# Second edge layer of a graph network: destination rows spread by a backward scan instead of gathered

## The chip, the cores and the metric

One core of one Trainium2 chip. The metric is the device time of one launch in microseconds (us). The kernel before was timed three times: median 6531.28 us, from 6530.24 to 6546.5 us.

## The reference, cut to what matters

100,000 nodes with 96 features in f32, 50,000 edges. The edges come **sorted by destination**, so all edges into one node stand next to each other (a run). Four graph layers follow one another, each in the form `x = x + layer(relu(norm(x)))`; the fourth is a stack of three convolutions with one norm and one skip around it. The first two layers have an MLP on every edge; the second is the one that changes here:

```python
# second edge layer, h = relu(layernorm(x))
e = jnp.concatenate([h[src], h[dst]], axis=-1)
e = jax.nn.relu(e @ Wm1 + bm1) @ Wm2 + bm2
e = e * drop_mask                                  # edge_attr_96
m = jax.ops.segment_sum(e, dst, num_segments=n)
z = jnp.concatenate([h, m], axis=-1)
h_new = jax.nn.relu(z @ Wu1 + bu1) @ Wu2 + bu2
```

`h[dst]` is one row per run: every edge of a run has the same destination row, normed in the same way.

## The kernel before, in words

All work goes in **groups** of 512 rows: four tiles of 128 partitions by 96 features. Nodes that no edge points to need no messages; they are handled for all nodes alike in a **node pass** (phase `dn`, 196 groups), which writes its rows to the tables `t1` and `t2` behind row `E_PAD` = 50,176. Nodes with edges are handled in edge order: 98 groups of 512 edges, in each layer. The table rows below `E_PAD` belong to edges: the row at the **last** edge of a run holds the right state of its destination node after each layer (the sum over a run is complete there), the rows at other edges hold values that nobody looks up. So to find a node's current row one needs a translation from node number to table row, `info_d` (row, and degree factor).

The stages in order:

- Counting (0 to 515 us): degrees and the translation table are built.
- Node pass `dn` (515 to 2105 us): per group a dense load, norm, MLP, norm, MLP, three stores. Beside it, on GpSimd, `info_gather` looks up two groups of 128 edges per step: four gathers of 8 bytes per row from `info_d` into `got` (two for the sources, `which` 0, two for the destinations, `which` 1) and two gathers of source rows of `x`. The found numbers are kept in `found`.
- First edge layer `e0` (2105 to 2927 us), not changed in its work.
- Second edge layer `e1` (2927 to 3935 us), lines 657 to 677 (GpSimd), 793 to 850 (ScalarE), 963 to 1045 (TensorE), 1324 to 1401 (VectorE). Per group eight gathers on GpSimd: four of source rows into `xs`, four of destination rows into `xd`, both from `t1`.
- Four convolution passes `conv` (3935 to 6548 us), each bound to gathers of its own.

Within `e1` a group j runs through: moments of `xs` and `xd` (`edge_moments`), `rstd` and `nmr` by eleven tiny instructions (`roots`), ScalarE norms into `hs` and `hd`, TensorE transposes both (`tr`, L973 and L978), ScalarE copies them out of PSUM into `hsT` and `hdT` (`evac_s`, `evac_d`), TensorE computes the hidden layer (`hid`, L990 from `hsT`, L992 from `hdT`), ScalarE applies relu (L828), TensorE makes messages (L1007), VectorE multiplies with the mask (`times_drop`, L1349), TensorE turns the messages (L1015), VectorE sums runs by a forward scan (`sums`, L1317; the factor `goes` is 1 where an edge has the destination of the edge before it, and 0 where a run begins), TensorE computes the update (`upd_z`, L1023 from `hdT`, L1024 from `aggT`; `upd_u`, L1031), and VectorE adds it to the edge's own row `xn` (`new_x`, L1381), which SyncE loads from `t1` in edge order (`res`).

The order on each engine is fixed by `pipelined(engine, n, stages)`: in step i an engine does its stages in the order of the list, each for group i minus its lag. No scheduler moves anything; an instruction waits for its semaphores and everything behind it on its engine waits with it. Before, `e1` has these lists: TensorE `hid` 1, `upd_z` 3, `turn_messages` 2, `messages` 1, `upd_u` 3, `tr` 0; ScalarE `evac_d` 1, `hidden` 1, `update_act` 3, `norms` 0, `evac_s` 0; VectorE `times_drop` 2, `new_x` 4, `edge_moments` 0, `of_round` (roots) 0, `sums` 2; GpSimd and SyncE run ahead as far as buffers allow (`xs`, `xd`, `xn`: six, `goes`, `drop`: three).

Of the kernel before, what the change touches and what calls it, by code (L numbers as in the profile page):

```python
# [6 lines left out]
F16 = mybir.dt.float16  # L7
# [4 lines left out]
P = 128  # L12
D = 96
# [78 lines left out]
def half(g):  # L92

    return g.c // GT % 2
# [24 lines left out]
def build(nc, a, out):  # L119
    with ExitStack() as ctx:  # L120
# [12 lines left out]
        goes_d = dram("goes_d", (E_PAD,), F16)  # L133
# [44 lines left out]
        at = sb("at", [P, 7, ET], I32)  # L178
        found = sb("found", [P, 2, ET, 2])
# [4 lines left out]
        off = sb("off", [HI, 1])  # L184


        idx = sb("idx", [P, 2, 2, GT * G], I32)
        idx_out = sb("idx_out", [P, 2, GT * G], I32)
        got = sb("got", [P, 2, 2, GT * GI, 2])
# [28 lines left out]
        goes = sb("goes", [P, 3, GE], F16)  # L218
# [48 lines left out]
        idx_step = sem("idx_step")  # L267
        rows_found = sem("rows_found")
# [26 lines left out]
        def more(name, k, by):  # L295
# [6 lines left out]
                        got=(2, 2 * GI * GT, GT), kept=(2, 1, GT), xs=(6, GI, 1), c_out=(6, 1, 1)))  # L302
        dn["root"] = Count(sem("root_dn"))
        gathered = dict(idx_in=(2, 1, GT), xs=(6, G, 1), goes=(3, 1, 1), x_out=(3, 1, 1))
        edge_slots = dict(gathered, xd=(6, G, 1), attr=(3, 1, 1))
        e0 = Phase(EG, dict(mx=1, norm_s=1, norm=1, tr_s=1, tr=1, evac_s=1, evac=1, hid_g=1, hid=1, act_g=1, act=1,
                            tok_g=1, tok=1, gate=1, msg=1, agg=1, z=1, g=1, u=1, y=1, my=1, norm_y=1, yx=1, xb=1, xr=1),
                   {name: edge_slots[name] for name in edge_slots if name != "xs"} | dict(x_in=(6, 1, 1)))
# [55 lines left out]
        def _(sp):  # L364
# [5 lines left out]
            sp.wait_ge(pad_set, 3)  # L370
# [10 lines left out]
            sp.wait_ge(scratch_out, 64)  # L381
            sp.dma_start(st_p[:], dstp[0:E_PAD].rearrange("(p t) -> p t", t=ET)).then_inc(prev_in, 16)
# [26 lines left out]
            sp.dma_start(goes_d.rearrange("(p t) -> p t", t=ET), st_goes[:]).then_inc(goes_out, 16)  # L409
# [6 lines left out]
            def idx_columns(ph, g, n, per, planes):  # L416
                k = per * (GT if g.turn is not None else min(GT, n - g.j))
                sp.dma_start(idx[:, half(g), 0:planes.stop - planes.start, 0:k], at[:, planes, bass.ds(g.j * per, k)])\
                    .then_inc(ph["idx_in"][half(g)].sem, 16)

            def info_idx(g):
                if g.c % GT == 0:
                    need(sp, dn["got"][half(g)], freed(g, 6, 2 * GI * GT))
# [5 lines left out]
                    idx_columns(dn, g, NG, GI, slice(0, 2))  # L429

            def info_keep(g):
                last = is_last_group(g, NG)
                if g.c % GT == GT - 1 or last:
                    n = g.c % GT + 1
                    need(sp, dn["got"][half(g)], freed(g, 6, 2 * GI * GT) + 16 * 2 * GI * n)
                    sp.sem_inc(sp_turn, 1)
                    sp.dma_start(found[:, :, bass.ds((g.j - n + 1) * GI, n * GI), :].rearrange("p w e c -> p w (e c)"),
                                 got[:, half(g), :, 0:n * GI, :].rearrange("p w e c -> p w (e c)"))\
# [35 lines left out]
            def gather_idx(ph, planes):  # L474
# [1036 lines left out]
```

## Time and profile before

| | |
|---|---|
| runs | 6531.28 us median, 6530.24 to 6546.5 |
| span of the profiled execution | 6548.3 us (the page gives no other time of it) |
| PE, weight load | 4333.9 us busy (66%), 2863.0 us (44%) |
| VectorE | 3928.1 us (60%) |
| ScalarE | 3505.9 us (54%) |
| GpSimd | 4163.7 us (64%), 4323 instructions |
| DMA | 620.32 MB, mean 95 GB/s |

No engine is busy throughout, because the stages have different limits. Read one stage at a time: a table of windows, one per stage, then who waits for whom in that stage, then the timeline of one or two groups. A stage is bound by the engine that waits for nothing there; "issue" as the releaser of a wait means that the engine was only between two of its own instructions. PEclk is the granted TensorE clock as a share of 2.4 GHz; it has two levels, 1.00 and 0.50, and a mean between them tells how the time was shared. TensorE's f32 products are issued as two instructions each, so "x8" in its rows are four products.

### The profile page before, as it was taken

Reading aid. Unit: us, or ns where it says so; the run is one execution under the profiler, and the core shown is the slowest. Engines: PE = TensorE matmul, PEld = TensorE weight load, DVE = VectorE, ACT = ScalarE, POOL = GpSimd, SP = SyncE. Lnnn points to the kernel's source line nnn. Section 1 sums busy time; section 2 is a strip of 40 time slices with the busy share of each in tenths; the row PEclk is TensorE's granted clock in tenths of the full one; section 3 lists DMA queues with packets and bytes.
Section 4 is the critical chain, followed back from the end, with each engine's and each line's share of the span. In section 5 each row is a group of like instructions: output and inputs, shape, how many; then the busy total and the mean of one; then the engine's idle time right before and its main releaser. Section 6 shows DMA issues by size and latency. Waiting matters only on the chain. (4 is left out here: it accounts for less than half of the span.)

```text
span 6548.3 us, 106418 instructions
## 1 busy us (share of the span) xinstructions
PE 4333.9 (66%) x19614; PEld 2863.0 (44%) x19614; DVE 3928.1 (60%) x12722; ACT 3505.9 (54%) x8822; POOL 4163.7 (64%) x4323
## 2 busy tenths in 40 slices
PE   5777888888887999978788884554555555222222
PEld 2224655655664444434444443443444444222222
DVE  5666777777776888875555555665665443222222
ACT  6996888888886999975555552222222222111110
POOL 0006777777775544437777767775775776777777
PEclk9997888898888999987888885555555555555555
DMA  0003444444444333434444444554444999333332
GB/s 16 0 0 90 124 126 127 125 128 125 124 124 119 93 96 93 96 72 100 111 107 111 107 100 120 136 134 96 104 104 90 103 104 100 62 62 66 70 66 58
DMA packets 1058872, 620.32 MB, mean 95 GB/s; under 512 B 831285, under 2 KB 1004609, under 8 KB 1058778
## 3 DMA queue, kind: packets, MB, share of 16 engines
q1 hardware_dynamic: 920794, 450.66, 25.2%
q0 software_dynamic: 137984, 168.67, 17.2%
q14 instruction: 67, 0.55, 0.0%
q8 instruction: 27, 0.44, 0.0%
HBM read 368.86 MB, written 251.78 MB: 95 GB/s over the span
## 5 line engine op out<-in xcount | busy, mean ns | idle before, releaser
L629 POOL DMA_INDIRECT xs<-t,idx x1176 | 1110.2, 944 | 528.4 <-issue 349.1
L629 POOL DMA_INDIRECT got<-info_d,idx x784 | 788.9, 1006 | 776.7 <-issue 750.1
L1048 PE MATMUL bank<-ident,msg 128*96 128x128 f32 (+1 forms) x1568 | 424.8, 426 | 1047.0 <-ACT msg L872 872.6
L1055 PE MATMUL bank<-w,aggT 96*128 96x96 f32 (+1 forms) x3136 | 770.2, 426 | 400.8 <-DVE aggT L1317 400.5
L629 POOL DMA_INDIRECT xs<-c,idx x784 | 749.8, 956 | 296.5 <-issue 233.0
L1055 PEld LDWEIGHTS bank<-w,aggT 96*128 96x128 f32 (+1 forms) x3136 | 704.4, 329 | 503.0 <-issue 422.9
L872 ACT ACTIVATE msg<-xs,now 128x96 f32<-128x96 f32 x784 | 229.4, 363 | 1279.8 <-DMA xs<-c,idx 840.0
L1048 PEld LDWEIGHTS bank<-ident,msg 128*96 128x96 f32 (+1 forms) x1568 | 285.7, 216 | 1113.3 <-ACT msg L872 738.5
L1317 DVE TENSOR_TENSOR_SCAN aggT<-goes,aggT,bank 96x512 f32<-96x512 f16 (+1 forms) x490 | 621.2, 1268 | 102.3 <-PE bank L1015 34.6
L629 POOL DMA_INDIRECT xd<-in_x_dram,idx x392 | 374.9, 956 | 415.8 <-DVE xn L1366 228.3
L725 ACT ACTIVATE hd<-xd,nmr,rstd 128x96 f32<-128x96 f32 x1568 | 599.3, 455 | 27.5 <-DVE nmr L1206 27.5
L1462 DVE SCALAR_TENSOR_TENSOR y<-bank,now,rows 128x96 f32<-128x96 f32 x392 | 97.2, 311 | 699.0 <-PE bank L1055 699.0
L711 POOL DMA_INDIRECT out_dram<-xn,idx_out x392 | 390.0, 995 | 119.3 <-issue 119.0
L629 POOL DMA_INDIRECT xs<-in_x_dram,idx x392 | 377.3, 962 | 119.5 <-issue 118.6
L629 POOL DMA_INDIRECT xd<-t,idx x392 | 369.9, 944 | 119.5 <-issue 119.5
L1462 DVE SCALAR_TENSOR_TENSOR xn<-bank,now,rows 128x96 f32<-128x96 f32 x784 | 194.5, 311 | 406.7 <-PE bank L1055 394.5
L899 PE MATMUL bank<-xd,hot_hi 128*128 128x392 f16 x1568 | 324.0, 328 | 124.3 <-ACT hot_hi L737 116.0
L1117 DVE TENSOR_SCALAR xd<-iota_lo,lo_of 128x784 f16<-128x784 f16 x784 | 297.0, 421 | 143.1 <-PE bank L899 143.0
L725 ACT ACTIVATE hs<-xs,nmr,rstd 128x96 f32<-128x96 f32 x784 | 300.6, 456 | 135.2 <-DVE nmr L1206 135.0
L1231 DVE BATCH_NORM_STATS2 mv<-xs 128x6 f32<-128x192 f32 x392 | 122.2, 353 | 415.8 <-issue 217.0
L912 PE MATMUL bank<-hdT,uw 96*96 96x512 f32 x392 | 253.9, 734 | 175.8 <-ACT hdT L770 175.8
L932 PEld LDWEIGHTS bank<-uw,u 97*128 97x128 f32 x1568 | 279.0, 218 | 178.3 <-ACT u L775 109.2
(189 smaller groups left out, 10436.4 us busy)
## 6 DMA issues: line engine op xcount, KB each, us to landing
t<-xo SPq DMA_DIRECT2D x392, 192.0 KB
t<-xn SPq DMA_DIRECT2D x294, 192.0 KB, 2.2
goes<-goes_d SPq DMA_DIRECT2D x392, 128.0 KB
xd<-in_x_dram SPq DMA_DIRECT2D x196, 192.0 KB, 2.5
out_dram<-oo SPq DMA_DIRECT2D x196, 192.0 KB, 2.4
xd<-t SPq DMA_DIRECT2D x196, 192.0 KB, 3.5
c<-xn SPq DMA_DIRECT2D x196, 192.0 KB
x_src<-xs SPq DMA_DIRECT2D x196, 96.0 KB
```

The lines of the kernel that those rows point to most:

```text
L629: nc.gpsimd.indirect_dma_start(out=into, out_offset=None, in_=table, in_offset=bass.IndirectOffsetOnAxis(ap=indices, axis=0)).then_inc(don ...
L711: nc.gpsimd.indirect_dma_start(out=out[:, :], out_offset=bass.IndirectOffsetOnAxis(ap=idx_out[:, half(g), col + c:col + c + 1], axis=0), i ...
L725: ins = nc.scalar.activation(into[:, c, :], x[:, c, :], ACT.Relu, bias=nmr[:, b, q, c:c + 1], scale=rstd[:, b, q, c:c + 1])
L872: ins = nc.scalar.activation(msg[:, g.at(2), c, 0:D], xs[:, g.at(6), c, :], ACT.Relu, scale=scale[:, col + c:col + c + 1])
L899: ins = nc.tensor.matmul(bank[1 + 2 * which + side][0:HI, 0:SIDE], hot_hi[:, g.at(2), which, 0:HI], hot_lo[:, g.at(2), which, side * SIDE: ...
L912: nc.tensor.matmul(into, w, x, start=True, stop=True).then_inc(done.sem, 1)
L932: nc.tensor.matmul(to, u1[:, g.at(2), e], uw2[:], start=True, stop=False)
L1048: ins = nc.tensor.transpose(bank[g.at(2)][0:m, c * P:(c + 1) * P], msg[:, g.at(2), c, 0:m], ident[:])
L1055: ins = nc.tensor.matmul(tok(bank[2 + g.at(2)], m)[:, c, :], aggT[0:m, g.at(3), c * P:(c + 1) * P], w2[:] if k == 0 else w3[:, k - 1, :], ...
L1117: nc.vector.tensor_scalar(hot_lo[:, g.at(2), which, :], iota_lo[:], lo_of[:, which, bass.ds(g.j, 1)], None, ALU.is_equal).then_inc(hot, 1)
L1317: nc.vector.tensor_tensor_scan(aggT[0:m, s, :], goes[0:m, s, :], source(g), aggT[0:m, before, GE - 1:GE], ALU.mult, ALU.add)\
L1462: ins = nc.vector.scalar_tensor_tensor(out=to, in0=u[:, c, 0:D], scalar=now[:, half(g), 1, col + c:col + c + 1], in1=rows[:, 1 + k, :], op ...
```

## The change

The destination look-ups and gathers go. Since the edges are sorted, the state of the destination of every edge of a run is the table row at the run's last edge, and that row is among the rows that `e1` loads in edge order anyway (`xn`, the row to which the update is added). So:

- `edge_moments` and the second half of `norms` read `xn` instead of `xd`. After `rstd` is made, a twelfth instruction multiplies it with `is_last`, and `nmr` is made from the product: relu(0·x + 0) = 0, so `hd` has the normed row at the last edge of each run and zeros elsewhere.
- After the transpose, `evac_d` on ScalarE is gone; VectorE's new stage `spread` writes `hdT` by a scan that goes **backward** over the 512 edges of the group: `hdT[i] = goes[i+1] * hdT[i+1] + bank[i]`. A run's row is thus carried back to all its edges. The scan starts from `carry[:, j]`, the normed row with which a run that goes on past the end of group j has to start.
- `carry` (96 by 98) is made once before `e1`: one gather of 98 rows of `info_d` at the start of the node pass, one gather of 98 rows of `t1` before the first gather of `e1`, moments and roots over 98 rows (`end_pass`: 13 small VectorE instructions), one norm, one transpose, one copy.
- `goes` in `e1` is loaded one column wider (513). In SyncE's list `res_load` moves to lag 1 (it was part of `edge_load`, lag 3) and `goes_load` from lag 5 to lag 2.
- GpSimd has four gathers per group in `e1` (before eight), and four per step in the node pass (before six); its wait for a free buffer is now on `norm_s` alone. Index tiles shrink to one plane; `found` and `got` too.

VectorE in the middle of `e1`, one step from its last roots instruction on, before (`mv` are the moments, `bank` a PSUM bank, `aggT` the running sums):

```order
L1206 SCALAR_TENSOR_TENSOR nmr<-mv,rstd 128x12
L1317 SCALAR_TENSOR_TENSOR aggT<-goes,aggT,bank 96x512
L1349 TENSOR_TENSOR msg<-bank,drop 128x4x96
L1381 TENSOR_TENSOR xo<-xn,bank 128x384
L1231 BN_STATS mv<-xs 128x6 x2
L1231 BN_STATS mv<-xd 128x6 x2
L1184 TENSOR_SCALAR var<-mv 128x12
```

and with the change:

```order
L1247 SCALAR_TENSOR_TENSOR rstd<-sq,root 128x12
L1252 TENSOR_TENSOR rstd<-rstd,is_last 128x4
L1254 SCALAR_TENSOR_TENSOR nmr<-mv,rstd 128x12
L1367 SCALAR_TENSOR_TENSOR aggT<-goes,aggT,bank 96x512
L1420 TENSOR_TENSOR msg<-bank,drop 128x4x96
L1451 TENSOR_TENSOR xo<-xn,bank 128x384
L1280 BN_STATS mv<-xs 128x6 x2
L1280 BN_STATS mv<-xn 128x6 x2
L1402 SCALAR_TENSOR_TENSOR hdT<-goes,carry,bank 96x512
L1228 TENSOR_SCALAR var<-mv 128x12
```

Moved: one small instruction (L1252) stands ahead of `nmr`, the moments read `xn`, and the scan `hdT` of the group before (L1402) stands between the moments and the roots of the new group. This listing names both scans SCALAR_TENSOR_TENSOR; in the trace they are TENSOR_TENSOR_SCAN.

ScalarE in the middle of `e1`, one step, before (`m` is the hidden layer's relu, `u` the update's):

```order
L809 ACTIVATE hsT<-bank 96x512
L814 ACTIVATE hdT<-bank 96x512
L828 ACTIVATE m<-bank,bias 96x512
L840 ACTIVATE u<-bank,bias 96x512
L725 ACTIVATE hs<-xs,nmr,rstd 128x96 x4
L725 ACTIVATE hd<-xd,nmr,rstd 128x96 x4
L809 ACTIVATE hsT<-bank 96x512
```

and with the change:

```order
L755 ACTIVATE hs<-xs,nmr,rstd 128x96 x4
L755 ACTIVATE hd<-xn,nmr,rstd 128x96 x4
L846 ACTIVATE hsT<-bank 96x512
L865 ACTIVATE m<-bank,bias 96x512
L877 ACTIVATE u<-bank,bias 96x512
L755 ACTIVATE hs<-xs,nmr,rstd 128x96 x4
L755 ACTIVATE hd<-xn,nmr,rstd 128x96 x4
```

Moved: the copy `hdT` is gone, so nothing of ScalarE stands between `hsT` and `m`; `u` stays ahead of the two norms `hs` and `hd`.

The diff, cut to its core:

```diff
-        goes_d = dram("goes_d", (E_PAD,), F16)
+        goes_d = dram("goes_d", (E_PAD + 1,), F16)
...
# SyncE
+            sp.dma_start(end_dst[:], dstp[1:1 + E_PAD].rearrange("(g e) -> g e", e=GE)[:, GE - 2:GE]).then_inc(ends_in, 16)
...
-                    if ph is e1:
-                        sp.dma_start(xn[:, g.at(6), :, :], edge_view(t1, first)).then_inc(ph["res"][g.at(6)].sem, 16)
+                def res_load(g):
+                    need(sp, ph["xr"], g.j - 5)
+                    sp.sem_inc(sp_turn, 1)
+                    sp.dma_start(xn[:, g.at(6), :, :], edge_view(t1, g.j * GE)).then_inc(ph["res"][g.at(6)].sem, 16)
...
+                if ph is e0:
+                    stages = [(gather_idx(ph, plane), 0), (xs_load, 1), (edge_load, 3), (goes_load, 5), (edge_store, done)]
+                else:
+                    stages = [(gather_idx(ph, plane), 0), (res_load, 1), (goes_load, 2), (edge_load, 3), (edge_store, done)]
# GpSimd
+            nc.gpsimd.indirect_dma_start(
+                out=end_info[:], out_offset=None, in_=info_d[:, :],
+                in_offset=bass.IndirectOffsetOnAxis(ap=end_dst[:, 1:2], axis=0)).then_inc(ends_found, 16)
...
-                for which in range(2):
-                    for c in range(col, col + GI):
-                        gather(got[:, half(g), which, c, :], info_d[:, :], idx[:, half(g), which, c:c + 1],
-                               dn["got"][half(g)])
+                for c in range(col, col + GI):
+                    gather(got[:, half(g), c, :], info_d[:, :], idx[:, half(g), c:c + 1], dn["got"][half(g)])
...
+                    nc.gpsimd.indirect_dma_start(
+                        out=end_x[:], out_offset=None, in_=t1[0:E_PAD, :],
+                        in_offset=bass.IndirectOffsetOnAxis(ap=end_at[:, 0:1], axis=0)).then_inc(end_rows, 16)
...
-                    need(pool, ph["norm"], g.j - 5)
+                    need(pool, ph["norm"] if ph is e0 else ph["norm_s"], g.j - 5)
...
-                    for c in range(G if ph is e1 else 0):
-                        gather(xs[:, g.at(6), c, :], t[:, :], idx[:, half(g), 0, col + c:col + c + 1], ph["xs"][g.at(6)])
-                    which = 1 if ph is e1 else 0
+                    into, done = (xd, ph["xd"]) if ph is e0 else (xs, ph["xs"])
                     for c in range(G):
-                        gather(xd[:, g.at(6), c, :], t[:, :], idx[:, half(g), which, col + c:col + c + 1], ph["xd"][g.at(6)])
+                        gather(into[:, g.at(6), c, :], t[:, :], idx[:, half(g), col + c:col + c + 1], done[g.at(6)])
# ScalarE
-                    normed(hd[:, g.at(6), :, :], xd[:, g.at(6), :, :], g.at(3), 1).then_inc(ph["norm"].sem, 1)
+                    normed(hd[:, g.at(6), :, :], (xd if first else xn)[:, g.at(6), :, :], g.at(3), 1)\
+                        .then_inc(ph["norm"].sem, 1)
...
-                    pipelined(act, EG, [(evac_d, 1), (hidden, 1), (update_act, 3), (norms, 0), (evac_s, 0)])
+                    pipelined(act, EG, [(hidden, 1), (update_act, 3), (norms, 0), (evac_s, 0)])
# VectorE
+                if masked is not None:
+                    part, mask = masked
+                    v.tensor_tensor(part, part, mask, ALU.mult).then_inc(count.sem, 1)
+                    need(dve, count, before + 11)
...
+                def spread(g):
+                    need(dve, ph["tr"], g.j + 1)
+                    need(dve, ph["goes"][g.at(3)], landed(g, 3))
+                    need(dve, ph["z"], g.j - 5)
+                    dve.sem_inc(dve_turn, 1)
+                    nc.vector.tensor_tensor_scan(hdT[0:D, g.at(6), ::-1], goes[0:D, g.at(3), 1:GE + 1][:, ::-1],
+                                                 bank[1][0:D, ::-1], carry[:, bass.ds(g.j, 1)], ALU.mult, ALU.add)\
+                        .then_inc(ph["evac"].sem, 1)
...
-                    stages = [(times_drop, 2), (new_x, 4), (edge_moments, 0), (of_round, 0), (sums, 2)]
+                    stages = [(times_drop, 2), (new_x, 4), (edge_moments, 0), (spread, 1), (of_round, 0), (sums, 2)]
```

## Rows read from the trace of the kernel before

**Rows 1.** Windows, one per stage: start:end, length, busy us (instructions), PEclk, DMA, GB/s
```profile
515.00:2105.00 1590.00, 1338.46 (x7056) 942.01 (x7056) 1194.30 (x4356) 1278.69 (x3137) 1166.19 (x1176) 0.86 0.43 123
2105.00:2927.00 822.00, 716.50 (x2744) 351.28 (x2744) 709.16 (x2305) 755.56 (x1764) 374.85 (x392) 0.98 0.38 91
2927.00:3935.00 1008.00, 813.93 (x3528) 472.45 (x3528) 515.10 (x1765) 527.50 (x1176) 739.85 (x784) 0.84 0.43 106
3935.00:4480.00 545.00, 290.97 (x1174) 250.01 (x1174) 353.10 (x1239) 144.04 (x392) 369.83 (x392) 0.50 0.54 130
```

**Rows 2.** Groups of GpSimd, second edge layer, 2990 to 3830 us: busy, mean ns, idle
```profile
L629 POOL DMA_INDIRECT xd<-t,idx x336 | 317.1, 944 | 102.4 <-issue 102.4
```

**Rows 3.** Timeline: both ends of the second edge layer
```profile
2927.21 0.94 POOL L629 DMA_INDIRECT xs<-t,idx  x1 [70.67 <-DMA idx<-at]
...
2938.70 0.63 DVE L1231 BATCH_NORM_STATS2 mv<-xs 128x6 f32<-128x192 f32 x2 [14.51 <-DMA xd<-t,idx]
...
3909.46 0.63 DVE L1231 BATCH_NORM_STATS2 mv<-xs 128x6 f32<-128x192 f32 x2 [5.48 <-issue]
...
3935.54 0.94 POOL L629 DMA_INDIRECT xs<-t,idx  x1 [29.84 <-DMA idx<-at]
```

**Rows 4.** Waits in the second edge layer, 2990 to 3830 us: total us, times, longest
```profile
DVE mv L1231 <- DMA xd<-t,idx: 146.4, 35, 5.7
```

**Rows 5.** Waits in the node pass, 700 to 1900 us
```profile
DVE mv L1231 <- PE bank L933: 198.6, 149, 4.1
...
POOL got L629 <- DMA found<-got: 18.0, 8, 4.9
```

**Rows 6.** Waits of the DMA queue SP in the same stretch
```profile
SPq L443 <- DVE xn L1258: 496.2, 126, 7.5
SPq L428 <- DMA xs<-in_x_dram,idx: 89.1, 47, 2.6
```

**Rows 7.** Timeline, node pass: the first product of two groups in succession
```profile
1202.69 1.10 PE L912 MATMUL bank<-hdT,uw 96*96 96x512 f32 x2 [1.12 <-ACT hdT L770]
...
1210.04 1.10 PE L912 MATMUL bank<-hdT,uw 96*96 96x512 f32 x2 [1.12 <-ACT hdT L770]
```

**Rows 8.** Timeline, second edge layer at full clock: start, length, engine, instruction, count
```profile
3410.99 0.69 ACT L840 ACTIVATE u<-bank,bias 96x512 f32<-96x512 f32 x1 [1.03 <-PE bank L1024]
...
3411.57 1.53 ACT L725 ACTIVATE hs<-xs,nmr,rstd 128x96 f32<-128x96 f32 x4
...
3411.57 1.28 DVE L1317 TENSOR_TENSOR_SCAN aggT<-goes,aggT,bank 96x512 f32<-96x512 f16 x1 [0.17 <-PE bank L1015]
...
3413.00 1.53 ACT L725 ACTIVATE hd<-xd,nmr,rstd 128x96 f32<-128x96 f32 x4
...
3414.59 0.64 PE L978 MATMUL bank<-ident,hd 128*96 128x128 f32 x4 [0.79 <-ACT hd L725]
...
3415.34 0.59 ACT L814 ACTIVATE hdT<-bank 96x512 f32<-96x512 f32 x1 [0.33 <-PE bank L978]
...
3416.08 1.02 PE L992 MATMUL bank<-hdT,wm 96*96 96x512 f32 x2
...
3417.79 1.02 PE L1024 MATMUL bank<-aggT,wu 96*96 96x512 f32 x2
...
3418.65 0.60 PE L1015 MATMUL bank<-ident,msg 128*96 128x128 f32 x4
...
3418.93 0.68 ACT L840 ACTIVATE u<-bank,bias 96x512 f32<-96x512 f32 x1 [1.03 <-PE bank L1024]
...
3419.09 1.03 PE L1007 MATMUL bank<-wm,m 97*128 97x96 f32 x8
...
3419.96 1.06 PE L1031 MATMUL bank<-wu,u 97*128 97x96 f32 x8
```

**Rows 9.** Groups of VectorE, second edge layer, 2990 to 3830 us: a small instruction
```profile
L1206 DVE SCALAR_TENSOR_TENSOR nmr<-mv,rstd 128x12 f32<-128x12 f32 x84 | 14.3, 171 | 2.9
```

**Rows 10.** Timeline, second edge layer at half clock: a product of two instructions
```profile
2947.82 1.91 PE L992 MATMUL bank<-hdT,wm 96*96 96x512 f32 x2
```

More of the change, by code:

```diff
@@ L413, in _, with idx_columns @@
                 .then_inc(info_out, 16)
-            def idx_columns(ph, g, n, per, planes):
+            def idx_columns(ph, g, n, per, plane):
                 k = per * (GT if g.turn is not None else min(GT, n - g.j))
-                sp.dma_start(idx[:, half(g), 0:planes.stop - planes.start, 0:k], at[:, planes, bass.ds(g.j * per, k)])\
+                sp.dma_start(idx[:, half(g), 0:k], at[:, plane, bass.ds(g.j * per, k)])\
                     .then_inc(ph["idx_in"][half(g)].sem, 16)
@@ L649, in info_gather @@
                 for c in range(GI):
[L650 removed]
+                    gather(xs[:, g.at(6), c, :], a["x"][:, :], idx[:, half(g), col + c:col + c + 1], dn["xs"][g.at(6)])
             pipelined(pool, NG, [(info_gather, 0)])
@@ L702, in conv_gather @@
                     for c in range(G):
-                        gather(xs[:, g.at(6), c, :], t[:, :], idx[:, half(g), 0, col + c:col + c + 1], ph["xs"][g.at(6)])
+                        gather(xs[:, g.at(6), c, :], t[:, :], idx[:, half(g), col + c:col + c + 1], ph["xs"][g.at(6)])
                 def scatter(g):
@@ L795, in _ @@
                 w = P if first else D
+                if not first:
+                    act.wait_ge(end_step, 13)
+                    nc.scalar.activation(end_h[:], end_x[:], ACT.Relu, bias=end_s[:, 8, 0:1], scale=end_s[:, 7, 0:1])\
+                        .then_inc(end_normed, 1)
+                    act.wait_ge(end_turned, 1)
+                    nc.scalar.activation(carry[:], bank[7][0:D, 0:EG], ACT.Copy).then_inc(carried, 1)
                 def norms(g):
-                    need(act, ph["root"], ROOT * (g.j + 1))
+                    need(act, ph["root"], (ROOT if first else ROOT + 1) * (g.j + 1))
                     need(act, ph["tr_s"], g.j - 2)
@@ L965, in _ @@
                 w = P if first else D
+                if not first:
+                    pe.wait_ge(end_normed, 1)
+                    nc.tensor.transpose(bank[7][0:D, 0:EG], end_h[:], ident[0:EG, 0:EG]).then_inc(end_turned, 1)
+                    pe.wait_ge(carried, 1)
                 def tr(g):
@@ L1176, in pair_stats, with roots @@
                 return ins
-            def roots(stats, slots, readers, count, before):
+            def roots(stats, slots, ready, count, before, masked=None):
                 var_, guess_, sq_, res_, root_, r, n = slots
-                for sem_, value in readers:
+                for sem_, value in ready:
                     need(dve, sem_, value)
@@ L1320, in sums_of, with end_pass @@
                 return sums
+            def end_pass():
+                dve.wait_ge(end_rows, 16)
+                nc.vector.bn_stats(end_mv[:].rearrange("p c f -> p (c f)"),
+                                   end_x[:].unsqueeze(2).broadcast_to([EG, D, 2])).then_inc(end_step, 1)
+                dve.wait_ge(end_step, 1)
+                s = [end_s[:, i, :] for i in range(9)]
+                roots(end_mv[:], (s[0], s[1], (s[2], s[3]), (s[4], s[5]), s[6], s[7], s[8]), (), Count(end_step, 1), 0)
+                dve.wait_ge(end_step, 12)
+                nc.vector.tensor_copy(end_s[:, 6, :], end_s[:, 8, :]).then_inc(end_step, 1)
+                dve.wait_ge(carried, 1)
             for ph in (e0, e1):
@@ L1394, in _ @@
                     dve.wait_ge(idx_step, 2)
-                of_round = roots_of(ph, edge_state)
+                    end_pass()
+                of_round = roots_of(ph, edge_state, not first)
                 if first:
```

109 lines of the change are left out of this document (66 added, 43 removed).

## The prediction

> **What bounds the kernel now.** I read the windows first, one per stage [rows 1], because the whole-kernel shares (GpSimd 64%, TensorE 66%) belong to no stage. The change touches two of them: the node pass (515 to 2105 us) loses two of six look-ups per step, the second edge layer (2927 to 3935 us) loses four of eight gathers per group.
>
> Second edge layer: GpSimd is busy 739.85 us with 784 gathers in 1008 us. A gather takes 944 ns and is followed by 102.4/336 = 0.30 us of "issue" [rows 2], so 1.25 us each, eight per group: 10.0 us. The stage's pace is the same: first moments at 2938.70, last at 3909.46, 97 steps apart, 10.01 us each [rows 3]. GpSimd waits for nothing there, and VectorE waits for its gathers (146.4 us in 840 [rows 4]). So this stage is bound by gathers, and nothing else counts in it as long as it takes under 10 us per group.
>
> Node pass: here GpSimd looks saturated too. In 1200 us all that it is shown waiting for, besides its own issue, is the keeping of look-ups, 18.0 us [rows 5]. But nobody on the compute side waits for it: VectorE waits for TensorE (198.6 us), and SyncE, the only link between look-ups and dense loads, waits 496.2 us for VectorE and only 89.1 us for gathers, 2.6 us at most [rows 6]. At full clock a group takes 1210.04 - 1202.69 = 7.35 us, in a ring TensorE, ScalarE, TensorE [rows 7]; with the stage's clock of 0.86 that becomes the 7.9 us per step that 1590 us over 196 groups and some five steps of filling and draining give. GpSimd needs 6 x 1.25 = 7.5 us and more. It is a close second here, not the bound.
>
> **The change part by part.**
>
> Node pass: 2 x 196 = 392 look-ups off GpSimd, some 490 us of its time, hidden behind the ring above: I take 0. Bounds: if GpSimd set the pace after all, the pace can go down to 7.35 at best, (7.9 - 7.35) x 196 = -108 us; upward +15 us, the spread of the three runs (16 us), for a ring that meets the clock's falls at other moments. One look-up more at the start, 1.25 us: in the noise. First edge layer and the four convolutions: same work, 0.
>
> Second edge layer, the gathers: 4 x 1.25 = 5.0 us per group remain. They no longer bind, so the question is which ring is next. Sums per engine and group: ScalarE 527.5/98 = 5.4, less the copy L814 of 0.59 [rows 8], is 4.8 us. VectorE 515.1/98 = 5.3, plus a scan as long as its present one (1.28 [rows 8]) and a masked instruction of 0.17 plus 0.03 between [rows 9], is 6.8, some 7.2 with the gaps of the small ones. TensorE at full clock: two products of 512 columns start 1.71 apart (3416.08 to 3417.79), so four of them 3.42; a set of transposes 0.44 (3418.65 to 3419.09), three of them 1.32; a set of small products 0.87 (3419.09 to 3419.96), two of them 1.74; together 6.48 us [rows 8]. No engine alone comes near 10.
>
> But the engines are now in one ring that the gathers used to hide. The scan of group j-1 stands on VectorE ahead of the roots of group j, and it needs TensorE's transpose, which needs ScalarE's norms. On ScalarE the norms stand behind the update's activation u, and that waits for TensorE's update, which stands behind the second half of the hidden layer, which waits for the scan. One turn at full clock, all from rows 7:
> - scan done to L992: 0.1, a handoff (the others in these rows are 0.06 and 0.17)
> - L992 to start of u: 3418.93 - 3416.08 = 2.85
> - u to hs 3411.57 - 3410.99 = 0.58; hs to hd 1.43; hd 1.53
> - hd done to the transpose L978 0.06; the transpose 0.64; to VectorE 0.17
> - the backward scan 1.28
>
> Sum 8.64 us. The roots of the next group (12 x 0.2 = 2.4 us) run beside the first of these steps (0.1 + 2.85 + 0.58 = 3.53), so the twelfth instruction is free; it costs its 0.2 only if u came over 1 us sooner. Queued behind the waiting scan on VectorE are the roots, then sums, mask and add, which nobody needs before the turn is over.
>
> What the backward scan takes I don't see in this trace: nearest is the forward scan over the same 96 x 512 with f16 factors, from PSUM, 1.28. Bounds: 0.59, what ScalarE takes to copy the same bank [rows 8], and twice the forward scan, 2.6. I take 1.28, the row of the same instruction.
> The Trainium skill, Vector Engine (DVE) Microarchitecture Reference, section 5.1, lists how the engine streams an operand with a negative step among what has not been measured. So it gives no reason for another price, and none against one; no row here has such an operand.
>
> The clock: at 1.2 GHz TensorE's own work is 2 x 6.48 = 12.96 us (L992 takes 1.91 there against 1.02 [rows 8, 10]) and is itself the bound, over the 10.0 of today. Today's stage has granted clock 0.84, so a third of its time is at half clock, and the gathers' pace, with six buffers, swallows that. The new ring can't. What clock will it get? The stages give a scale, busy share of TensorE to clock [rows 1]: 0.87 to 0.98, 0.84 to 0.86, 0.81 to 0.84, 0.53 to 0.50. The new ring has 6.48 plus some 0.8 of tails in 8.64, 0.84: next to the node pass, on the side of the first edge layer. I take 0.88, that is 24% of the time at half clock. Pace: 1 / (0.76/8.64 + 0.24/12.96) = 9.39 us. Bounds: at 0.98 it is 8.76, at 0.80 it is 9.97.
>
> The ends: first gather to first moments 11.49 us today, less four gathers, 6.5; last moments to the next stage's first gather 26.1 [rows 3], kept. The carries: their gather needs no index load, GpSimd has been idle 70.67 us before [rows 3] and can start when the last rows are stored; 13 small instructions (2.7 us), a norm, a transpose and a copy follow beside group 0's gathers. I take 0, at worst +4 us. SyncE: the earlier loads of xn and goes have six and three buffers and land steps ahead; the list is no longer. 0.
>
> Sum: 6.5 + 97 x 9.39 + 26.1 = 943 us against 3935.54 - 2927.21 = 1008, so -65 us. On the profiled span, 6548.3 becomes 6483. That span stands 17 us over the median of the runs, near the slowest of them; I take the difference off the median: 6531 - 65 = 6466.
>
> **The rivals.**
> 1. The node pass was GpSimd's after all. For: its near lack of waits [rows 5]. Against: nobody waits for it [rows 6]. It would give half the bound, -50 us, on top: 6416.
> 2. The gain is eaten, within 20 us of before: a pace of 9.85 to 10.2, by a clock of about 0.8 or small handoffs that I missed (a microsecond per turn is enough, since the ring has some nine of them). For: a mean clock of 0.84 today. 6528.
> 3. Slower, by the clock: the ring has no cover, and each time the clock falls it pays in full. The point from which it decides: a pace over 10.06 (the 5 us won at the start shared over 97 groups), which is 42% of the time at half clock, a granted clock of 0.79. At 0.75 the pace is 10.37, the stage 1039 us, the kernel 6562; held at 0.50 as in the convolutions [rows 1] it would be 6.5 + 97 x 12.96 + 26.1 = 1290, 6813. Against: every stage with TensorE over 0.8 busy has 0.84 or more.
> The Trainium skill, TensorE: Matmul & The Clock Gate, section "A second HAM failure mode: psum-queue depth-cycling", says that short idle spells between groups of matmuls are enough to make the clock swing, and cost throughput. By that the new ring, with a wait in every turn, would go the way of this rival. Today's stage agrees with the page (0.84), the first edge layer hardly (0.98) [rows 1].
> 4. The backward scan takes twice the forward one: ring 9.92, with the same clock 10.51, +44 us, 6575. For: nothing but that it is not shown.
>
> **How the numbers follow.** Forecast (savings of 25 to 130 us by the ring's pace) 0.72, rival 1 0.10, rival 2 0.09, rival 3 0.05, rival 4 0.04. Time 6466. Range: down to the clock of 0.98 (97 x 8.76 + 32.6 = 882, -126: 6405) and a little of rival 1, 6395; up to the clock of 0.80 (-8) and a few us: 6525. A measurement of this kernel tells some 0.3%, 20 us, from no change. Faster 0.72 + 0.10 = 0.82; same 0.09; slower 0.05 + 0.04 = 0.09.
>
> **What would show it.** In the second edge layer: moments 8.7 to 9.7 us apart, 8.6 in stretches of full clock; four gathers per group with GpSimd now waiting for ScalarE's norms; VectorE's scan waiting for the transpose L978's successor, about 1 us per group; ScalarE's norms directly behind u; the backward scan at 1.3 us; granted clock 0.85 to 0.92. Node pass: 7.9 us per step as before, GpSimd at 5 us of it. Wrong: if the stage's clock is under 0.8, if the scan takes over 2 us, or if the node pass is over 20 us shorter.

## The result, and the profile after

| | median | runs |
|---|---|---|
| before | 6535.44 us | 6530.24 to 6546.5 (4) |
| with the change | 6982.68 us | 6971.87 to 6990.6 (4) |

The ratio is 1.0676, with an interval of [1.0659, 1.0694]: 447 us slower. The prediction was 6466 us, faster, with a range up to 6525. It was wrong in sign and in size. The profiled execution has a span of 6970.1 us.

The first view is again the table of windows, one per stage (start:end, length, then busy us and instructions of PE, PEld, DVE, ACT, POOL, then PEclk, DMA share, GB/s). These four rows answer to [rows 1]:

```profile
515.00:2088.00 1573.00, 1310.92 (x7056) 917.98 (x7056) 1189.86 (x4356) 1275.54 (x3137) 775.03 (x785) 0.88 0.41 124
2088.00:2910.00 822.00, 717.47 (x2744) 351.53 (x2744) 710.85 (x2305) 755.95 (x1764) 376.56 (x393) 0.98 0.38 90
2910.00:4355.00 1445.00, 942.90 (x3529) 499.98 (x3529) 641.66 (x1974) 462.62 (x1080) 370.05 (x393) 0.75 0.25 60
4355.00:4900.00 545.00, 291.56 (x1176) 250.62 (x1176) 352.98 (x1239) 144.05 (x392) 369.47 (x392) 0.50 0.53 130
```

The loss is in the third row, the second edge layer: 1445 us where it was 1008. The first edge layer and the convolutions have their old lengths. In this stage GpSimd is busy for 370 us, half of before, as meant. No engine is busy for more than 943 of the 1445 us, so the engines wait for each other. The granted clock fell from 0.84 to 0.75.

Who waits for whom, 3000 to 4200 us (engine, line, what it waited for, us in total, times, longest); the old row is [rows 4]:

```profile
POOL xs L654 <- DMA idx<-at: 745.8, 25, 31.1
ACT m L865 <- PE bank L1033: 628.5, 81, 8.8
...
PE bank L1033 <- DVE hdT L1402: 361.7, 80, 5.6
DVE xo L1451 <- DMA t<-xo: 351.6, 80, 5.6
DVE aggT L1367 <- PE bank L1056: 283.5, 81, 4.2
```

Read such a list from the wait that is not an engine of the ring. GpSimd now waits for its indices, so gathers are far from the bound. ScalarE waits for TensorE, TensorE for VectorE's backward scan, VectorE for TensorE. The odd one is VectorE waiting for `t<-xo`, **a store**, in each group, 4.4 us on average (351.6/80). In this stage of the kernel before no engine waits for a store.

The timeline of one turn shows why (start us, length, engine, line, operation; in brackets the idle time before it and what ended it). `SPq` rows are DMAs that SyncE issues:

```profile
3407.67 1.28 DVE L1367 TENSOR_TENSOR_SCAN aggT<-goes,aggT,bank 96x512 f32<-96x512 f16 x1 [3.42 <-PE bank L1056]
...
3409.17 0.33 SPq L537 DMA_DIRECT2D goes<-goes_d  x1
...
3409.68 0.37 SPq L526 DMA_DIRECT2D drop<-in_edge_attr_dram  x1
3410.33 0.40 SPq L543 DMA_DIRECT2D t<-xo  x1
...
3413.89 0.56 DVE L1451 TENSOR_TENSOR xo<-xn,bank 128x384 f32<-128x384 f32 x1 [4.49 <-DMA t<-xo]
...
3415.41 1.26 DVE L1402 TENSOR_TENSOR_SCAN hdT<-goes,carry,bank 96x512 f32<-96x512 f16 x1
...
3416.73 2.02 PE L1033 MATMUL bank<-hdT,wm 96*96 96x512 f32 x2 [4.39 <-DVE hdT L1402]
...
3418.54 1.92 PE L1064 MATMUL bank<-hdT,wu 96*96 96x512 f32 x2
...
3420.25 1.91 PE L1065 MATMUL bank<-aggT,wu 96*96 96x512 f32 x2
...
3421.96 1.06 PE L1056 MATMUL bank<-ident,msg 128*96 128x128 f32 x4
...
3423.42 1.28 DVE L1367 TENSOR_TENSOR_SCAN aggT<-goes,aggT,bank 96x512 f32<-96x512 f16 x1 [4.06 <-PE bank L1056]
```

The ring, 15.75 us in this turn: the forward scan, then SyncE issues `goes`, `drop` and the store; 3.56 us after the store's issue it has landed and `new_x` writes `xo`; the moments and the backward scan are behind it on VectorE; then TensorE's products, at half clock (1.9 to 2.0 us each, 1.02 at full), and the next forward scan.

**Why the store is late.** SyncE works through its list in order. In its step i it loads `goes` for group i-2, and `goes_load` first waits until the forward scan of group i-5 is done (three `goes` buffers). VectorE does that scan at the end of its own step i-3. Behind it in the list, in the same step i, stands the store of group i-9. `new_x` of group i-6 needs that store landed, since `xo` has three buffers, and VectorE does it in its step i-2, behind the scan with only the mask's product (`times_drop`) between them. So between the scan and `new_x` lie three issues of SyncE, the store's the last of them, and a landing, in every step. With the old lag of 5, `goes_load` waited for a scan three steps earlier, so the store was not tied to the scan just ahead of `new_x`. SyncE's own waits in the same stretch show the tie; L535 stands directly behind the condition in `goes_load`:

```profile
SPq L535 <- DVE aggT L1367: 714.1, 81, 9.6
```

That is 8.8 us of each turn (714.1/81) in which nothing behind it in SyncE's list can be issued.

The operation about which I was least sure is as forecast (lines view, 3000 to 4200 us: busy, mean ns, idle before):

```profile
L1367 DVE TENSOR_TENSOR_SCAN aggT<-goes,aggT,bank 96x512 f32<-96x512 f16 x81 | 103.3, 1276 | 283.5 <-PE bank L1056 283.5
L1402 DVE TENSOR_TENSOR_SCAN hdT<-goes,carry,bank 96x512 f32<-96x512 f16 x80 | 100.7, 1259 | 0.0
```

### The profile page after: what moved, and what is told of

Its sections match the earlier page's. It is cut to its first block and busy times, and to the rows that moved or that the text cites. A ratio compares the mean times of both kernels' runs of the same rounds, so it can differ in the third digit from the quotient of the medians.

```text
span 6970.1 us, 105980 instructions
## 1 busy us (share of the span) xinstructions
PE 4438.8 (64%) x19615; PEld 2866.6 (41%) x19615; DVE 4050.6 (58%) x12933; ACT 3426.2 (49%) x8726; POOL 3403.3 (49%) x3541
## 5 line engine op out<-in xcount | busy, mean ns | idle before, releaser
L1367 DVE TENSOR_TENSOR_SCAN aggT<-goes,aggT,bank 96x512 f32<-96x512 f16 (+1 forms) x490 | 621.1, 1268 | 402.2 <-PE bank L1056 329.8
L654 POOL DMA_INDIRECT got<-info_d,idx x392 | 382.8, 976 | 620.0 <-DMA found<-got 515.6
L755 ACT ACTIVATE hd<-xd,nmr,rstd 128x96 f32<-128x96 f32 x1176 | 449.6, 455 | 27.1 <-DVE nmr L1254 27.1
L1033 PE MATMUL bank<-hdT,wm 96*96 96x512 f32 x196 | 193.6, 1090 | 413.0 <-DVE hdT L1402 413.0
L865 ACT ACTIVATE m<-bank,bias 96x512 f32<-96x512 f32 x98 | 66.9, 683 | 727.7 <-PE bank L1033 727.7
L969 PE MATMUL bank<-uw,u 97*128 97x96 f32 x1568 | 346.4, 306 | 6.3 <-ACT u L805 3.1
```

The costliest lines, as they stand in the source:

```text
L654: nc.gpsimd.indirect_dma_start(out=into, out_offset=None, in_=table, in_offset=bass.IndirectOffsetOnAxis(ap=indices, axis=0)).then_inc(don ...
L755: ins = nc.scalar.activation(into[:, c, :], x[:, c, :], ACT.Relu, bias=nmr[:, b, q, c:c + 1], scale=rstd[:, b, q, c:c + 1])
L969: nc.tensor.matmul(to, u1[:, g.at(2), e], uw2[:], start=True, stop=False)
L1367: nc.vector.tensor_tensor_scan(aggT[0:m, s, :], goes[0:m, s, 0:GE], source(g), aggT[0:m, before, GE - 1:GE], ALU.mult, ALU.add)\
```

## The experiments

Theory A: the late store, tied to VectorE's forward scan by the moved `goes_load`, lengthens the ring; the clock falls in its pause. Theory B: the ring of the prediction with a low clock, rival 3, at a much higher price. The kernel before stood at 6538.41 us (13 runs) beside the first three kernels and the first reordering, at 6540.57 (7 runs) beside the next four, and at 6540.45 (7 runs) beside the last. Pace is 700 us over the groups in the window 3000 to 3700 us.

### The store one step earlier

```diff
-            edge_phase(e1, t2, 2, 9)
+            edge_phase(e1, t2, 2, 8)
```

> The changed kernel with one number altered: in the second edge layer SyncE stores group j's rows at lag 8 of its list instead of lag 9. Theory A (the late store): with goes_load at lag 2 SyncE's step i can't begin before VectorE's forward scan in its step i-3, so the store of group g-3 leaves only after the scan just ahead of new_x(g), which waits for that store because there are three xo buffers (351.6 us in 1200 on VectorE). One lag less lets it leave a whole step earlier, the wait goes to nearly nothing, and the ring of the prediction is left: 8.6 us at full clock, 9.0 to 9.6 on the mean, stage 900 to 970 us, kernel 6420 to 6490 us. Theory B (the ring itself is long because TensorE's clock falls with its pauses): the wait goes away but the pace stays over 11 us, kernel over 6620 us. If neither is touched: about 6980 us.

Measured: 6479.6 us (6464.13 to 6498.87), ratio 0.9904 [0.9873, 0.9935]. The store of group j now stands a step earlier, ahead of the `goes_load` that ties it. One number takes 503 us away and turns 7% slower into 1% faster. The wait for `t<-xo` is gone from the list of waits. A turn at full clock, from this kernel's timeline:

```profile
3400.72 1.28 DVE L1402 TENSOR_TENSOR_SCAN hdT<-goes,carry,bank 96x512 f32<-96x512 f16 x1 [0.19 <-issue]
3402.05 1.10 PE L1033 MATMUL bank<-hdT,wm 96*96 96x512 f32 x2 [0.81 <-DVE hdT L1402]
...
3404.98 0.68 ACT L877 ACTIVATE u<-bank,bias 96x512 f32<-96x512 f32 x1 [1.11 <-PE bank L1065]
...
3407.00 1.53 ACT L755 ACTIVATE hd<-xn,nmr,rstd 128x96 f32<-128x96 f32 x4
...
3408.58 0.64 PE L1019 MATMUL bank<-ident,hd 128*96 128x128 f32 x4 [0.79 <-ACT hd L755]
...
3409.48 1.28 DVE L1402 TENSOR_TENSOR_SCAN hdT<-goes,carry,bank 96x512 f32<-96x512 f16 x1 [0.75 <-PE bank L1019]
```

This is the ring of the prediction, step by step: 8.76 us where 8.64 was worked out. SyncE still waits in front of `goes_load` (3000 to 3700 us), but no engine of the ring waits for what stands behind it (GpSimd waits for its indices, off the ring):

```profile
SPq L535 <- DVE aggT L1367: 478.0, 74, 9.2
```

The stage runs from 2927.11 (gather of the carries) to 3874.57 (next stage's first gather), 947.5 us against 943 forecast.

### The late store in the kernel before

The two lists, shortened:

```diff
-[(edge_load, 3), (goes_load, 5), (edge_store, done)]
+[(goes_load, 2), (edge_load, 3), (edge_store, done)]     # in e1 alone
```

> The kernel before with only SyncE's list for the second edge layer altered: goes_load at lag 2 and first, instead of lag 5 (the loads of xn stay in edge_load). Theory A: VectorE gets the same wait for the stored rows, some 4.4 us per group, but the pace of before is 10 us and VectorE has about 4.7 us of idle time in it, so most is absorbed: forward scan 1.3, store through SyncE and DMA 4.9, add 0.5, moments 1.2, roots 2.3, together 10.2 us per group, kernel 6535 to 6590 us, with a row VectorE xo waiting for DMA t<-xo of 3 to 5 us per group. Theory B (the lag has no part in it): 6535 us and no such row.

Measured: 6649.58 us (6645.78 to 6665.94), ratio 1.0171 [1.0128, 1.0215]. Slower than I had expected (at most 6590), but the direction and the row are those of A: without any part of the backward scan, the moved load alone costs 111 us. Its wait (3000 to 3700 us) and one turn:

```profile
DVE xo L1381 <- DMA t<-xo: 339.4, 63, 6.1
```

```profile
3403.33 1.28 DVE L1317 TENSOR_TENSOR_SCAN aggT<-goes,aggT,bank 96x512 f32<-96x512 f16 x1 [0.29 <-issue]
3404.88 0.35 SPq L516 DMA_DIRECT2D goes<-goes_d  x1
3405.64 0.38 SPq L509 DMA_DIRECT2D drop<-in_edge_attr_dram  x1
3406.12 0.45 SPq L511 DMA_DIRECT2D xn<-t  x1
3406.84 0.40 SPq L522 DMA_DIRECT2D t<-xo  x1
3410.27 0.55 DVE L1381 TENSOR_TENSOR xo<-xn,bank 128x384 f32<-128x384 f32 x1 [5.21 <-DMA t<-xo]
...
3414.23 1.28 DVE L1317 TENSOR_TENSOR_SCAN aggT<-goes,aggT,bank 96x512 f32<-96x512 f16 x1
```

Here three issues stand between scan and store, one more than in the changed kernel (the load of `xn`, 0.72 us from its issue to that of the store), and this one the expectation had not counted. The turn is 10.9 us. That just passes the gathers' 10.0: the wait is 5.4 us per group on average (339.4/63), the stage loses some 1.1 us per group, and the gathers' cover soaks up the rest. The changed kernel has no such cover.

### Six buffers for `xo`

```diff
-    need(dve, ph["x_out"][g.at(3)], freed(g, 3))
-    nc.vector.tensor_tensor(xo[:, g.at(3), :, :], xn[:, g.at(6), :, :], tok(bank[7]), ALU.add)
+    need(dve, ph["x_out"][g.at(6)], freed(g, 6))
+    nc.vector.tensor_tensor(six(g), xn[:, g.at(6), :, :], tok(bank[7]), ALU.add)
```

`six(g)` is one of the three `xo` tiles or one of the three `oo` tiles of the node pass, which are free here; the store reads the same tile. All lists stay as in the change.

> The changed kernel with SyncE's list as changed (store at lag 9, goes at lag 2), but six buffers for the second edge layer's results instead of three (the three idle ones of the node pass are taken too). Theory A: the store is as late as before, but new_x(g) now waits for the store of group g-6, three steps back, so the wait is gone: same as with the store at lag 8, kernel 6420 to 6490 us. If it is not the buffer but something that SyncE's order delays (loads of xn, goes or the mask), it stays over 6700 us.

Measured: 6479.36 us (6460.35 to 6503.04), ratio 0.9896 [0.9853, 0.9939]. The store stands where it stood in the change, but nobody needs it in that step: the same gain by another way. What cost the time is the wait for a free buffer, and nobody waits for the stored data.

### `goes_load` at lag 3, the store untouched

```diff
-    stages = [(gather_idx(ph, plane), 0), (res_load, 1), (goes_load, 2), (edge_load, 3), (edge_store, done)]
+    stages = [(gather_idx(ph, plane), 0), (res_load, 1), (goes_load, 3), (edge_load, 3), (edge_store, done)]
```

> The changed kernel with goes_load at lag 3 instead of 2, the store still at lag 9, still three buffers. Theory A as it now stands: the store is late because goes_load(i-2) ties SyncE's step i to VectorE's forward scan in step i-3; with goes_load(i-3) the tie is to the scan in step i-4, and SyncE is held only by res_load(i-1), that is by new_x in step i-3, early in that step. The store of g-3 then leaves about 8 us before new_x(g) and has 5 us to land: same as with the store at lag 8, 6450 to 6500 us. If instead the move of the loads of xn (res_load at lag 1) were what delays SyncE, the wait stays at 3 to 4 us per group and the kernel over 6700 us.

Measured: 6480.37 us (6466.67 to 6498.71), ratio 0.991 [0.9886, 0.9934], no wait for a store, with `res_load` still at lag 1. The cause is the lag of that one load together with the store behind it and its three buffers: each of the three, altered alone, takes the loss away. The backward scan can use a load one step later than the change gives it.

### Filler products, with the early store

```diff
+    nc.tensor.matmul(bank[3][0:D, 0:256], wm1[:, 0, :], before[...], start=True, stop=True)   # twice per group
```

One stands after the transpose of `hs`, one between the halves of the hidden layer. They write a bank that is not in use.

> Store at lag 8, and TensorE gets two extra products of 256 columns per group in pauses of the ring (one ahead of L1033, one between the two transposes), whose results nobody reads. Full-clock ring is 8.76 us in the trace of e1_store8, the mean pace 9.4 at a granted clock of 0.92. If the difference is the clock: it rises to 0.97 or more, pace 8.8 to 9.0, kernel 6420 to 6450 us. If it isn't the clock, TensorE has 0.9 us more work per group and the kernel gets slower or stays, 6480 to 6520 us.

Measured: 6415.47 us (6413.63 to 6419.12), ratio 0.9809 [0.9792, 0.9825], 64 us less than with the early store alone, with work added. Windows 3000 to 3700 us, first the early store, then with the fillers:

```profile
3000.00:3700.00 700.00, 590.15 (x2672) 334.62 (x2672) 483.01 (x1488) 350.07 (x818) 280.29 (x297) 0.92 0.38 95
```

```profile
3000.00:3700.00 700.00, 645.95 (x3179) 383.72 (x3178) 515.65 (x1593) 373.36 (x871) 302.40 (x321) 1.00 0.41 101
```

The granted clock goes from 0.92 to 1.00 and the pace from 9.4 to 8.75 us, which is the ring at full clock. So some 0.65 us of the early store's pace was the clock.

### Fillers in the late-store kernel

```diff
+    for _ in range(6):          # in the second kernel: range(11)
+        filler()                # before TensorE waits for the backward scan
```

and one after the transpose of `hs`. Everything else is the changed kernel.

> The changed kernel as given (store at lag 9, goes at lag 2), with TensorE kept busy in its pause: six extra products of 256 columns ahead of L1033 (2.6 us at full clock) and one between the transposes, results unread. The ring through the late store is, at full clock, forward scan 1.3, SyncE 1.4, store 3.5, add and moments 1.5, backward scan 1.3, TensorE to the next forward scan about 2.8 and 0.4: 12.2 us; the trace shows 14.6 at a clock of about 0.7. If the clock is a second cause beside the late store, this gives 12.2 to 13.2 us per group and 6740 to 6850 us in all; if the pace is the store's alone, or if the fill keeps the low clock and lengthens the ring, 6980 us or more.

Measured: 6908.79 us (6901.89 to 6921.39), ratio 1.0567 [1.0549, 1.0585]. That is between what the two theories said, so it settled nothing by itself. The granted clock is 0.86 (3000 to 3700 us). Its timeline shows why: the fillers end before the wait does, and the clock still falls in what is left of it in some turns.

```profile
3413.62 2.75 PE L1009 MATMUL bank<-before,wm 96*96 96x256 f32 x12
3418.62 2.02 PE L1040 MATMUL bank<-hdT,wm 96*96 96x512 f32 x2 [2.25 <-DVE hdT L1409]
```

So the same with eleven:

> The changed kernel with its late store left as it is, and eleven filler products of 256 columns per group on TensorE (written to an unused bank) between the first half of the hidden layer and the second, which waits for the backward scan, and one after the transposes of the source rows. The fillers take the place of TensorE's wait: with six of them 2.0 to 2.3 us of pause were left, five more at 0.43 us fill 2.15 us. Theory (the ring through the late store sets the pace, and the clock that falls in its pause adds to it): the ring from the forward scan to the second half of the hidden layer takes 9.3 us whatever the clock (forward scan, three issues of SyncE, store, addition, moments, backward scan), and from there to the next forward scan 3.44 us at full clock against 6.5 at half. With the clock held the pace is 12.7 us, the granted clock over 0.95, the kernel near 6770 us (6730 to 6820). Rival (the late store costs nearly all of it, and the clock only its part of a turn that is not in the ring): the pace stays over 14 us and the kernel over 6880. Third case: the fillers overrun the wait and the second half starts later: the pause is gone but the pace is over 13.5.

Measured: 6796.06 us (6779.98 to 6799.85), ratio 1.0381 [1.0353, 1.0409]; 6770 was expected. The window and one turn (its lines are 7 further down than in the change: L1040 is L1033, L1374 is L1367, L1458 is L1451, L1409 is L1402):

```profile
3000.00:3700.00 700.00, 677.70 (x3321) 450.46 (x3320) 358.87 (x1101) 260.53 (x608) 213.91 (x227) 1.00 0.28 70
```

```profile
3409.14 1.28 DVE L1374 TENSOR_TENSOR_SCAN aggT<-goes,aggT,bank 96x512 f32<-96x512 f16 x1 [1.35 <-PE bank L1063]
3410.64 0.34 SPq L537 DMA_DIRECT2D goes<-goes_d  x1
3411.15 0.37 SPq L526 DMA_DIRECT2D drop<-in_edge_attr_dram  x1
3411.80 0.40 SPq L543 DMA_DIRECT2D t<-xo  x1
...
3415.09 0.55 DVE L1458 TENSOR_TENSOR xo<-xn,bank 128x384 f32<-128x384 f32 x1 [4.23 <-DMA t<-xo]
...
3416.63 1.26 DVE L1409 TENSOR_TENSOR_SCAN hdT<-goes,carry,bank 96x512 f32<-96x512 f16 x1
...
3418.32 1.02 PE L1040 MATMUL bank<-hdT,wm 96*96 96x512 f32 x2
...
3421.68 1.28 DVE L1374 TENSOR_TENSOR_SCAN aggT<-goes,aggT,bank 96x512 f32<-96x512 f16 x1 [1.24 <-PE bank L1063]
```

The clock is held at 1.00, and the pace is 12.5 us. The late store is still there and now stands alone: scan to store issue 2.66, store to `new_x` 3.29, addition and moments 1.54, backward scan and the rest of the fillers 1.69, TensorE to the next scan 3.36, together 12.54. Only the last term was longer in the turn of the changed kernel by much: 6.69 there, at half clock.

### A shorter ring, first try

```diff
# with the early store
-    pipelined(act, EG, [(hidden, 1), (update_act, 3), (norms, 0), (evac_s, 0)])
+    pipelined(act, EG, [(hidden, 1), (norms, 0), (update_act, 3), (evac_s, 0)])
-    pipelined(pe, EG, [(hid, 1), (upd_z, 3), (turn_messages, 2), (messages, 1), (upd_u, 3), (tr, 0)])
+    pipelined(pe, EG, [(hid, 1), (upd_z, 3), (turn_messages, 2), (messages, 1), (tr, 0), (upd_u, 3)])
```

> Store at lag 8, and the ring cut: ScalarE does the two norms ahead of the update's activation, TensorE the two transposes ahead of the update's last product. Then the ring is scan, roots 2.4, norms 3.0, transpose 0.7, scan 1.3 and handoffs 0.4: 7.8 us at full clock. If the ring of the prediction holds (norms behind u), this is faster than the store at lag 8 alone by 0.5 to 0.9 us per group, 50 to 90 us, kernel 6360 to 6420 us. If the pace is set by something else (TensorE at half clock, stores), no difference within 20 us.

Measured: 6587.99 us (6580.14 to 6598.04), ratio 1.0072 [1.0053, 1.0092], where 6360 to 6420 was expected. I had freed the norms of the update, but put the update's product `upd_u` (L1072) behind the norms, and VectorE's `new_x` needs it. Moments and backward scan stand behind `new_x` in VectorE's list. Two rows of its timeline:

```profile
3407.46 1.03 PE L1072 MATMUL bank<-wu,u 97*128 97x96 f32 x8
3408.52 0.55 DVE L1451 TENSOR_TENSOR xo<-xn,bank 128x384 f32<-128x384 f32 x1 [0.87 <-PE bank L1072]
```

The wait is small (48.9 us in the window) and yet it is in the ring: TensorE now waits 2.03 us for the backward scan in every turn, a turn of this timeline takes 10.4 us, and the clock fell to 0.82. How much of the loss is the wait and how much the clock is not separated. It is the mistake of the prediction once more: an edit priced by what it frees, without reading what stands behind the moved stage.

### A shorter ring, second try

```diff
# as the first try, and
-    stages = [(times_drop, 2), (new_x, 4), (edge_moments, 0), (spread, 1), (of_round, 0), (sums, 2)]
+    stages = [(times_drop, 2), (edge_moments, 0), (spread, 1), (of_round, 0), (sums, 2), (new_x, 4)]
```

> Store at lag 8, norms ahead of u on ScalarE and transposes ahead of the update's last product on TensorE, as in e4, and on VectorE new_x moved to the end of the step, behind the forward scan. In e4 the trace showed VectorE's add (xo) waiting for the update's last product, now late, with moments and backward scan queued behind it. Theory: with the add out of the way the ring is scan 1.28, roots 2.5, norms 2.97, transpose 0.64 and handoffs 0.3 to 0.4, 7.7 us, another through the forward scan about 7.9; TensorE is busier and keeps its clock at 0.9 or more: pace 8.1 to 8.7 us, kernel 6350 to 6420 us. Rival: TensorE's clock falls again as in e4 (0.82), pace over 9.2, kernel 6460 us or more.

Measured: **6345.35 us** (6337.63 to 6352.26), ratio 0.9698 [0.9682, 0.9715]: faster than both kernels, 195 us under the kernel before. Its window and two backward scans in succession:

```profile
3000.00:3700.00 700.00, 627.76 (x3146) 372.90 (x3145) 559.57 (x1745) 411.30 (x963) 324.50 (x344) 1.00 0.46 110
```

```profile
3399.80 1.26 DVE L1402 TENSOR_TENSOR_SCAN hdT<-goes,carry,bank 96x512 f32<-96x512 f16 x1
...
3403.37 0.17 DVE L1254 SCALAR_TENSOR_TENSOR nmr<-mv,rstd 128x12 f32<-128x12 f32 x1
3404.55 1.28 DVE L1367 TENSOR_TENSOR_SCAN aggT<-goes,aggT,bank 96x512 f32<-96x512 f16 x1 [1.01 <-PE bank L1056]
...
3406.60 0.64 PE L1019 MATMUL bank<-ident,hd 128*96 128x128 f32 x4 [0.79 <-ACT hd L755]
...
3407.72 1.26 DVE L1402 TENSOR_TENSOR_SCAN hdT<-goes,carry,bank 96x512 f32<-96x512 f16 x1
```

A turn is 7.92 us, the clock 1.00 with no filler. VectorE's only wait of size is now ahead of the forward scan, 1.0 us in this turn, and TensorE's is ahead of L1019, 0.8 us: both are nearly without a pause, so either would bind soon if the ring got shorter still. The pace fell by some 1.4 us against the early store alone (9.4). The fillers gave 8.75 for the old ring at full clock, so an estimate from the two is 0.8 us for the shorter ring and 0.6 for the clock; no run separates them.

## Why the prediction was wrong, step by step

- **SyncE's list** ("the earlier loads of xn and goes have six and three buffers and land steps ahead; the list is no longer. 0"): **this is the step that failed.** Both halves of the sentence are true, and neither prices the move. The loads are not late, and no engine is shown waiting for one of `xn` or `goes`; the wait in front of the moved load is what SyncE's later instructions are queued behind, and one of them is the store that frees `xo`. It cost some 500 us: 6982.68 against 6479.6 with that tie cut. The numbers needed were all readable: the lag, the condition in `goes_load`, the three buffers of `xo`.
- **The split of those 503 us.** At full clock in both, by fillers, late against early store is 6796.06 - 6415.47 = 381 us, 3.9 us in each of 97 turns (12.54 less some 8.7). The rest, about 122 us, is more clock lost: 187 us with the late store (6982.68 - 6796.06) against 64 with the early one (6479.6 - 6415.47). The eleven fillers themselves overrun the wait: L1040 starts 0.43 us after the backward scan ends, where 0.06 is the handoff in the changed kernel. By that estimate some 35 us of the 381 are the fillers', so the store's part is nearer 345 us and the clock's nearer 155.
- **The new ring**, 8.64 us at full clock: 8.76 measured with the early store. Right. (Its terms are read from [rows 8]; the prediction says rows 7.)
- **The backward scan**, 1.28 (bounds 0.59 to 2.6): 1.26, and 1.28 with the early store. Right. The Trainium skill, Vector Engine (DVE) Microarchitecture Reference, section 5.1, leaves the price of a negative step open; here it has none that shows.
- **The clock**, 0.88 and a pace of 9.39: with the early store 0.90 over 2910 to 3880 us and 9.34 us between moments ((3844.71 - 2938.33)/97). Right for the ring that I had in mind, and in part luck: 0.88 was a choice between stage means from 0.84 to 0.98, and from 3000 to 3700 us the same ring had 0.92 with the early store and 0.87 with six buffers. In the kernel as changed it is 0.75, under the 0.8 that the prediction named as a sign of being wrong. The sign was rival 3's, not its mechanism: at 0.75 it gave 10.4 us per turn, and 14.5 came ((4322.17 - 2919.34)/97). The Trainium skill, TensorE: Matmul & The Clock Gate, section "A second HAM failure mode: psum-queue depth-cycling", says that short idle spells between groups of matmuls make the clock swing and cost throughput. The runs agree (0.92 becomes 1.00 when two fillers shorten pauses of 0.65 to 0.81 us to under 0.4, for 64 us), but that is the smaller part of what came.
- **The ends**, 6.5 and 26.1, carries 0 to +4: gather of the carries to first moments 10.4 (2908.93 to 2919.34), last moments to the next stage 32.6 after the change, 29.9 with the early store. Together +8 to +10 us. In the early-store kernel this is made up in part by the pace (97 x 0.05 = 5 us less), so 947.5 against 943 is closer than its terms are.
- **Node pass**, 0: its window is 1573 us against 1590. In the nine profiles without the look-ups the second edge layer's first gather starts at 2905.7 to 2927.1 us, on average at 2913.8; in the two with them at 2927.2 and 2921.2. So 392 look-ups less may be worth some 10 us, inside that scatter, and not more. GpSimd's wait there (700 to 1900 us) rose from 18.0 us [rows 5] to 414.7 us, idle time that it gave to nobody.
- **GpSimd in the second edge layer** was to wait for ScalarE's norms. It waits for its index loads instead, in the early-store kernel too (294.0 of 700 us, for the norms 2.7); they are in SyncE's list like the store. That is off the ring: no wait of VectorE's moments for a gather is shown from 3000 to 3700 us.
- **Sum**: with the one tie cut the kernel is 59 us faster than before (6479.6 against 6538.41); -65 was forecast. The other terms were right within some 10 us, and the prediction was still 517 us off: here one chain that closes through a DMA queue outweighed every duration in the sum.

The chances were wrong too. No rival named a DMA queue, though the diff shows the move in SyncE's list.

## What to carry to other kernels

When a load is moved to an earlier step of an in-order queue, read what it waits for and list what stands behind it in that step, stores first; ask for each store which buffer it frees and who writes that buffer next. A prefetch that waits for the consumer's last step ties every later transfer of its queue to that step. Whether this costs anything depends on who waits for those transfers: with the early store SyncE still waits in front of `goes_load` for 6.5 us per group (478.0/74), and no engine of the ring waits for what stands behind it. And when a stage loses its bound (here the gathers), the waits that it used to cover must be priced without cover: the same tie costs 111 us in the kernel before and some 500 in this one.

## What the runs showed of the hardware

- From its issue to the instruction that its landing releases, a store of 192 KB took 3.29 to 3.56 us; the profile's median to landing in this stage of the changed kernel is 3.2 us. That is over a quarter of the 12.5 us turn. The Trainium skill, DMA: Bandwidth & Descriptors, section "Anatomy of one DMA — SWDGE (gpsimd) path", gives some 2 us of fixed time to a DMA on GpSimd's path, most of it the confirmation that the last byte has landed. This store is issued by SyncE, and no run here splits its 3.2 us into such parts.
- TensorE's mean granted clock from 3000 to 3700 us, beside its pauses between products (read from 3400 to 3500 us): 0.75 with one of 4.2 to 5.1 us and most often one of 0.8 per turn (the change); 0.86 with one of 1.7 to 2.5 (six fillers); 0.82 with one of 2.03 (first reordering); 0.92 with two of 0.65 to 0.81 (early store) and 0.87 with much the same two (six buffers); 1.00 where fillers left none over 0.4 us. With the second reordering it stayed at 1.00 without any filler, though one pause of 0.79 us per turn was left; so the length of the pauses alone does not tell what the clock does. More work on TensorE made the kernel faster by 64 us in one kernel and 187 in the other.
